# A chunked delta attention: its inverse's last corner closed a wave later, the gates' differences behind the attention rows, the fourth z part by another bank, the norm's product on ScalarE

## The chip, the cores and the metric

The kernel runs on one core of one Trainium2 chip. The metric is the device time of one execution in microseconds, the median of several runs. It computes four small transformer layers in one launch, all in fp32, and only the last layer's attention, here called the delta stage, is touched by the change.

## The reference, cut to what matters

The hidden state has 2 x 512 tokens of 256 features. The delta stage has 16 key heads with two value heads each, dimension 128, and works on blocks of 128 tokens where the reference takes 64:

```python
qkvz = hidden_states @ W_qkvz               # per key head: q 128, k 128, v 2x128, z 2x128
qkv_c = silu(causal_conv(qkv, taps=4))      # per channel
beta = sigmoid(b); g = -exp(A_log) * softplus(a + dt_bias)
# per chunk, per value head:
g_cum = cumsum(g); decay = exp(tril(g_cum[:, None] - g_cum[None, :]))
attn = solve_triangular(I - L, I)           # L = -(k beta) k^T * decay, strictly lower
v_new = attn @ (v beta) - attn @ (k beta exp(g_cum)) @ state
out = (q exp(g_cum)) @ state + ((q k^T) * decay) @ v_new
state = state * exp(g_last) + (k exp(g_last - g_cum))^T @ v_new
# after it, per value head:
xf = out * silu(z); xf = xf * rsqrt(mean(xf*xf) + eps) * norm_weight
y = xf @ W_out                              # summed over heads, added into x
```

## The kernel before, in words

Five engines run programs of their own that meet only at semaphores. The delta stage is one software pipeline of waves: W = 64, wave w is chunk c = w mod 4 (CH = 4 blocks of 128 tokens) of key head h = w // 4, and it covers PR = 4 problems at once (2 batches x 2 value heads). Each engine's loop body (from L2341 for TensorE) is an order written out by hand. In body w before the change:

- for wave w+2, two ahead: `make_scores` (L2087, q and k against k, into bank BK), `turn_values` (L2098) and `turn_keys` (L2104) into bank BT; on VectorE `make_low` (L2635, differences of the gates' sums, from rows that SyncE broadcasts, `load_gates`, L1964), `make_v0` (L2650), `make_at` (L2641), `make_qg` (L2655); on ScalarE `make_decay` (L2409) and `grow` (L2415) are the exponentials, `make_values` and `make_keys` (L2424) the copies.
- `spread` on SyncE (L1970 to L1984) stores v0 and hands its 16x16 diagonal blocks to GpSimd; GpSimd's `substitute` (L2585 to L2598) inverts them in some thirty small steps; `gather` (L1993, L1999) brings them back a wave later.
- for wave w the inverse is put together from those blocks: `widen` (L2663), `join_a` (L2115), `close_wa` (L2671), `close_a` (L2127, L2131), `join_b` (L2140), `close_b` (L2150, L2152) in 32x32 tiles, then `join_c` (L2160) and `close_c` (L2169) for the last 64x64 corner. ScalarE's `copy_whole` (L2445) takes the finished bank BZ to `inv`.
- for wave w-1: `recall` (L2180) with `make_right` (L2690), `ask` (L2203), `solve` (L2192) with `new_values` (L2450), `grow_state` (L2218) with `carry` (L2712; not after a head's last chunk, and recall and ask not in its first), `answer` (L2209), then `gated` (L2700, xf), `square` (L2458), `reduce` (L2719) and on GpSimd `root` (L2567) and `normed` (L2573).
- for wave w-2: `turn_out` (L2229), `copy_out` (L2465), `project_out` (L2242), `add_out` (L2725).
- between them lie parts: the projections of the next head, eight q, k, v parts (L2043) and four z parts (L2053), `parts_of(w)` of them in a wave: 3, 3, 2, 4 for c = 2, 3, 0, 1. They go to banks BG and BK in turn. `conv` (L2618, L2621) and `silu` (L2396) make the next head's q, k, v from them; ScalarE drains z parts by a Silu (L2390).

SyncE's queue in body w: for c = 1, 2 the next weights (`load_qkv` L1818; `load_z` L1822 and `load_out` L1826), then `load_gates(w+3)`, `spread(w+2)`, `gather(w+1)`. Each issue waits in order.

Of the kernel before, what the change touches and what calls it, by code (L numbers as in the profile page):

```python
# [13 lines left out]
ALU = mybir.AluOpType  # L14
# [3 lines left out]
P = 128  # L18
# [1763 lines left out]
def delta_and_looked_up(nc, ps, d, x, xn, norm, looked_up):  # L1782
# [8 lines left out]
    FIRST_ORDER = (1, 0, 2, 3)  # L1791
    F_TILES = WF * B
# [9 lines left out]
    with Stage(nc, "a3") as s:  # L1802
# [50 lines left out]
        wc, z_half, t_half = (s.buf(n, [P, PR, P // 2]) for n in ("wc", "z_half", "t_half"))  # L1853
        inv = s.buf("inv", [P, 2, PR, P])
        at, qg, v_row, k_row = (s.buf(n, [P, 4, PR, P]) for n in ("at", "qg", "v_row", "k_row"))
        state, rest, v_new = (s.buf(n, [P, PR, P]) for n in ("state", "rest", "v_new"))
        xf, sq, xnorm, out_t = (s.buf(n, [P, PR, P]) for n in ("xf", "sq", "xnorm", "out_t"))
# [3 lines left out]
        f_gated = [of[:, :, :].rearrange("p r t -> p (r t)") for of in (xf, xnorm, state, rest)]  # L1861
# [90 lines left out]
        bg_parts = [part for w in range(-2, W + 2) for part in parts_of(w)[0::2]]  # L1952

        with nc.Block() as block:

            @block.sync
            def _(sp):
# [50 lines left out]
                for w in range(-2, W):  # L2008
# [28 lines left out]
            def _(pe):  # L2037
# [9 lines left out]
                def project_z(g, n, to):  # L2047
                    if n == 0:
                        pe.wait_ge(wz_loaded, 16 * g + 16)
                    for i in range(2):  # L2050
                        tt = 2 * n + i
# [6 lines left out]
                def part(w, n):  # L2058
# [3 lines left out]
                    if n % 2 == 0:  # L2062
# [3 lines left out]
                    elif n == 1:  # L2066
                        pe.wait_ge(v0_ready, PR * (w + 3))
                        pe.wait_ge(at_ready, w + 3)
                    else:
                        wait_part(pe, parts[n - 2])  # L2070
                    g, t = parts[n]
                    if t < 8:
                        project(g, t, (BG, BK)[n % 2])
                    else:
                        project_z(g, t - 8, (BG, BK)[n % 2])

                def make_scores(w):
                    before = parts_of(w - 3)
                    if before:
                        wait_part(pe, before[len(before) // 2 * 2 - 1])  # L2080
# [38 lines left out]
                def close_a(w):  # L2119

                    pe.wait_ge(wa_ready, w + 1)
                    if w >= 1:
                        pe.wait_ge(inv_ready, w)
# [32 lines left out]
                def join_c(w):  # L2156

                    pe.wait_ge(th_ready, w + 1)
                    for r in range(PR):
                        mm = pe.matmul(upper(BW)[SECOND, r, :], v0[FIRST, w % 3, r, SECOND], t_half[FIRST, r, :],  # L2160
                                       start=True, stop=True)
                    mm.then_inc(wc_psum, 1)

                def close_c(w):

                    pe.wait_ge(wc_ready, w + 1)
                    pe.wait_ge(zh_ready, w + 1)
                    for r in range(PR):
                        mm = pe.matmul(bank(BZ)[FIRST, r, SECOND], wc[SECOND, r, :], z_half[SECOND, r, :],  # L2169
                                       start=True, stop=True)  # L2170
# [855 lines left out]
```

## Time and profile before

| what | value |
|---|---|
| median of 3 runs | 2034.4 us (2026.47 to 2035.54) |
| the profiled execution | 2028.85 us, of which span 2027.0 us |
| granted TensorE clock, mean | 0.958 of full |
| TensorE busy | 1843.1 us, 91% |
| VectorE, ScalarE, GpSimd busy | 64%, 49%, 53% |
| DMA | 124.42 MB, mean 61 GB/s |

The span counts from the first to the last instruction; the execution's time has 1.8 us around it. The delta stage's loop begins at about 913 us. Busy time doesn't include semaphores and the issue of DMAs. The matmul ends are modelled, so the start of the next instruction is the safer reading of how long a run took.

### The profile page before, as it was taken

How to read it: one execution, taken by the hardware profiler on the slowest of the kernel's cores; microseconds unless marked ns; L12 is line 12 of the kernel's file. 1: busy time of each engine (PE TensorE's matmuls, PEld its weight loads, DVE VectorE, ACT ScalarE, POOL GpSimd, SP SyncE). 2: the span in 40 equal slices, each digit the busy share in tenths (PEclk: the TensorE clock that was granted, in tenths of full speed). 3: DMA queues.
4: the chain of work that ended last, by engine and by line, in shares of the span. 5: the costliest groups of instructions: out<-in, count | busy, mean ns of one | idle time of the engine just before them, and what ended most of it. 6: DMA issues, size and time to landing. Idle time of an engine off the chain costs nothing.

```text
span 2027.0 us, 45825 instructions
## 1 busy us (share of the span) xinstructions
PE 1843.1 (91%) x16855; PEld 1191.5 (59%) x16855; DVE 1287.5 (64%) x2490; ACT 995.4 (49%) x2433; POOL 1077.0 (53%) x2259
## 2 busy tenths in 40 slices
PE   7799997877899896898999999999999999999987
PEld 5422564432243574346777777777777777677775
DVE  2544564695578533627777777777777777777752
ACT  2375232215321452525656656665666566566643
POOL 0521222224100340126887787887878888888873
PEclk7899998998999796999999999999999999999999
DMA  6035422110010632202222222222222222222221
GB/s 157 1 116 156 108 46 53 52 62 1 1 44 7 176 116 88 40 14 56 53 53 64 64 54 54 64 63 55 49 60 54 53 64 64 54 53 64 44 45 32
DMA packets 231181, 124.42 MB, mean 61 GB/s; under 512 B 141360, under 2 KB 210513, under 8 KB 230705
## 3 DMA queue, kind: packets, MB, share of 16 engines
q1 hardware_dynamic: 225008, 111.20, 22.1%
q0 software_dynamic: 5952, 10.29, 2.2%
q8 instruction: 137, 2.24, 0.5%
q14 instruction: 84, 0.68, 0.1%
HBM read 87.94 MB, written 39.74 MB: 63 GB/s over the span
## 4 chain that ended last, share of the span: by engine, by line
PE 23%; POOL 20%; issue 6%; SPq 4%; ACT 3%; DMA 2%; DVE 2%; POOLq 0%; DVEq 0%; ACTq 0%
POOL a_term L2591 8%; POOL a_z L2595 8%; PE ps L2043 5%; PE ps L2053 3%; PE ps L2242 3%; SPq L1976 2%; POOL a_rstd L2567 2%; POOL a_xnorm L2573 2%; PE ps L2273 2%; DMA a_l<-a_v_dram 1%; SPq L1984 1%; PE ps L2229 1%; PE ps L2160 1%; PE ps L2209 1%; PE ps L2283 1%
## 5 line engine op out<-in xcount | busy, mean ns | idle before, releaser
L2591 POOL TENSOR_TENSOR a_term<-a_z,a_l 32x14 f32<-32x14 f32 (+6 forms) x896 | 342.8, 383 | 70.3
L2595 POOL TENSOR_TENSOR a_z<-a_z,a_term 32x14 f32<-32x14 f32 (+6 forms) x896 | 339.6, 379 | 70.2
L2621 DVE SCALAR_TENSOR_TENSOR a_qkv<-a_raw,a_taps,a_qkv 128x1024 f32<-128x1024 f32 x192 | 247.1, 1287 | 6.1
L2043 PE MATMUL ps<-all_xn,a_w_qkv 128*128 128x512 f32 x512 | 246.7, 607 | 0.0
L390 POOL DMA_INDIRECT f_rows<-a_row,a_slots x32 | 35.4, 1105 | 184.6 <-DVE a_of_tile L380 139.2
L2242 PE MATMUL ps<-a_out_t,a_w_out 128*128 128x256 f32 x512 | 130.7, 399 | 1.9 <-ACT a_out_t L2465 1.7
L2043 PEld LDWEIGHTS ps<-all_xn,a_w_qkv 128*128 128x128 f32 x512 | 89.2, 193 | 69.1 <-issue 67.3
L2386 ACT ACTIVATE a_raw<-ps 128x512 f32<-128x512 f32 x128 | 76.4, 598 | 108.2 <-PE ps L2043 107.5
L2053 PE MATMUL ps<-a_w_z,all_xn 128*128 128x256 f32 x512 | 122.6, 383 | 0.0
L2585 POOL COPY a_z<-a_l 32x256 f32<-32x256 f32 x64 | 27.1, 423 | 154.6 <-DMA a_l<-a_v_dram 154.4
L850 POOL DMA_INDIRECT f_sums<-a_y,a_xs x23 | 36.1, 1568 | 136.3 <-ACT a_y L799 133.4
L2242 PEld LDWEIGHTS ps<-a_out_t,a_w_out 128*128 128x128 f32 x512 | 93.8, 193 | 17.8 <-ACT a_out_t L2465 2.3
L2700 DVE SCALAR_TENSOR_TENSOR a_xf<-ps,a_zs 128x512 f32<-128x512 f32 x64 | 44.2, 690 | 91.0 <-POOL a_xnorm L2573 65.5
L2053 PEld LDWEIGHTS ps<-a_w_z,all_xn 128*128 128x128 f32 x512 | 93.6, 190 | 12.7 <-issue 1.2
L2650 DVE SCALAR_TENSOR_TENSOR a_v<-ps,a_gates,a_decay 128x128 f32<-128x128 f32 x256 | 71.6, 340 | 43.0 <-ACT a_decay L2409 43.0
L2450 ACT ACTIVATE a_v_new<-ps,a_gates 128x128 f32<-128x128 f32 x256 | 72.9, 367 | 45.7 <-PE ps L2192 45.7
L2635 DVE SCALAR_TENSOR_TENSOR a_low<-a_gc_rows,a_gates,a_floor 128x128 f32<-128x128 f32 x256 | 87.9, 403 | 1.6 <-DMA a_gc_rows<-a_g_dram 1.6
L630 PE MATMUL ps<-a_w,a_xt 128*128 x184 | 86.6, 593 | 0.6 <-ACT a_xt L779 0.6
L2567 POOL TENSOR_TENSOR a_rstd<-a_var,a_half 128x4 f32<-128x4 f32 x64 | 68.7, 1073 | 22.1 <-DVE a_var L2719 22.1
L772 ACT ACTIVATE a_probs<-ps 128x512 f32<-128x512 f32 x128 | 66.1, 602 | 23.9 <-PE ps L593 23.9
L2445 ACT ACTIVATE a_inv<-ps 128x512 f32<-128x512 f32 x64 | 38.3, 598 | 76.9 <-PE ps L2169 76.9
L2209 PE MATMUL ps<-a_v_new,a_at 128*128 128x128 f32 x512 | 74.8, 290 | 1.2 <-ACT a_v_new L2450 1.2
(331 smaller groups left out, 4304.7 us busy)
## 6 DMA issues: line engine op xcount, KB each, us to landing
a_gc_rows<-a_g_dram SPq DMA_DIRECT2D x64, 256.0 KB, 4.8
a_v_dram<-a_v SPq DMA_DIRECT2D x64, 256.0 KB
a_w<-in_f_w SPq DMA_DIRECT2D x24, 512.0 KB, 4.5
a_w_qkv<-in_a_w SPq DMA_DIRECT2D x16, 512.0 KB, 3.9
a_t_dram<-a_z SPq DMA_DIRECT2D x512, 8.0 KB
a_w_z<-in_a_w SPq DMA_DIRECT2D x16, 256.0 KB, 2.9
a_w_out<-in_a_wo SPq DMA_DIRECT2D x16, 256.0 KB, 3.1
a_v_off<-a_v SPq DMA_DIRECT2D x256, 4.0 KB
```

Source lines behind the costliest of these rows:

```text
L630: mm = pe.matmul(ps[:, bank + i % 2, :], xt[:, i % 2, k, :], w[:, bass.ds(e, 1), first + k * FF:first + (k + 1) * FF], start=k == 0, stop= ...
L2043: mm = pe.matmul(ps[:, to, :], w_qkv[:, k, mt * P:(mt + 1) * P], xn[:, k, b * T:(b + 1) * T], start=k == 0, stop=k == KC - 1)
L2053: mm = pe.matmul(ps[:, to, i * 256:(i + 1) * 256], xn[:, k, tt * P:(tt + 1) * P], w_z[:, k, :], start=k == 0, stop=k == KC - 1)
L2209: mm = pe.matmul(bank(BO)[:, r, :], at[:, w % 4, r, :], v_new[:, r, :], start=w % CH == 0 and r == 0, stop=r == PR - 1)
L2242: mm = pe.matmul(bank(BO)[:, B * m:B * (m + 1), :], w_out[:, v, m * P:(m + 1) * P], out_t[:, v::VPK, :], start=v == 0, stop=v == VPK - 1)
L2386: act.activation(raw[:, mt, b, TAPS - 1:], ps[:, of, :], ACT.Copy).then_inc(raw_ready, 1)
L2450: act.activation(v_new[:, r, :], bank(BR)[:, r, :], ACT.Copy, scale=gate(K_BETA, w, r)).then_inc(vnew_ready, 1)
L2567: pool.tensor_tensor(rstd[:, :], var[:, :], half[:, :], ALU.pow).then_inc(rstd_ready, 1)
L2591: pool.tensor_tensor(term[:, 0:j, j + 1:], z[:, 0:j, j:j + 1].broadcast_to([HP, j, n]), rows[:, j:j + 1, j + 1:].broadcast_to([HP, j, n]), ...
L2595: pool.tensor_tensor(z[:, 0:j, j + 1:], z[:, 0:j, j + 1:], term[:, 0:j, j + 1:], ALU.add).then_inc(sub_step, 1)
L2621: dve.scalar_tensor_tensor(to, rows, tap, to, ALU.mult, ALU.add).then_inc(conv_ready if j == TAPS - 1 else conv_step, 1)
L2635: dve.scalar_tensor_tensor(low[:, r, :], gc_rows[:, w % 2, r, :], gate(K_GC, w, r), floor[:, :], ALU.subtract, ALU.min).then_inc(low_ready, 1)
```

## The change

It does seven things. The closing of the last corner for wave w-1 is interleaved with the joining for wave w (`join_and_close_c`), and `copy_closed` takes only that quarter to `inv`; VectorE's `copy_halves` takes the two diagonal halves there. Everything that needs the inverse runs for w-2, and the output for w-3, so the loop has one more body. `part(w, 0)` stands behind `join_a` in the bodies that grow no state. Part 1 alone uses bank BK, the others BG, and the z parts' order is (0, 2, 1, 3). `make_low` runs for w+3 behind `make_at`. `normed` goes from GpSimd to four ScalarE activations, with xf doubled. `make_keys` goes ahead of `copy_wc`; `load_out` goes from c = 2 to c = 3; in c = 0 the conv's last tap goes to the head of the next body's.

```diff
+    Z_ORDER = (0, 2, 1, 3)
-        bg_parts = [part for w in range(-2, W + 2) for part in parts_of(w)[0::2]]
+        bg_parts = [parts[n] for parts in map(parts_of, range(-2, W + 2)) for n in range(len(parts)) if n != 1]
...
-                    if c == 2 and h >= 1:
+                    if c == 3 and 1 <= h:
                         sp.wait_ge(y_psum, CH * h)
                         load_out(sp, h)
...
+                def join_and_close_c(w):
+                    if made(w):
+                        pe.wait_ge(th_ready, w + 1)
+                    if made(w - 1):
+                        pe.wait_ge(wc_ready, w)
+                        pe.wait_ge(zh_ready, w)
+                    if made(w - 2):
+                        pe.wait_ge(inv_ready, w - 1)
                     for r in range(PR):
+                        if made(w):
+                            begun = pe.matmul(upper(BW)[SECOND, r, :], v0[FIRST, w % 3, r, SECOND],
+                                              corner[FIRST, r, :], start=True, stop=True)
+                        if made(w - 1):
+                            closed = pe.matmul(upper(BW)[FIRST, r, :], corner[SECOND, r, :],
+                                               inv[SECOND, (w - 1) % 2, r, SECOND], start=True, stop=True)
...
-                for w in range(W + 2):
-                    if made(w - 1):
-                        recall(w - 1)
+                for w in range(W + 3):
+                    if made(w - 2):
+                        recall(w - 2)
                     if made(w + 2):
                         make_scores(w + 2)
...
-                    part(w, 0)
+                    if w == W:
+                        join_and_close_c(w)
+                    grows = (w - 2) % CH != CH - 1
+                    if grows:
+                        part(w, 0)
                     if made(w):
                         join_a(w)
-                    if made(w - 1):
-                        grow_state(w - 1)
+                    if not grows:
+                        part(w, 0)
...
                     if made(w):
-                        join_c(w)
-                    if made(w - 2):
-                        project_out(w - 2)
+                        join_and_close_c(w)
+                    if made(w - 3):
+                        project_out(w - 3)
                     part(w, 3)
-                    if made(w):
-                        close_c(w)
...
-                def copy_whole(w):
+                def copy_closed(w):
                     act.wait_ge(c_psum, w + 1)
-                    act.activation(inv[:, w % 2, :, :], bank(BZ), ACT.Copy).then_inc(inv_ready, 1)
+                    act.activation(inv[FIRST, w % 2, :, SECOND], upper(BW)[FIRST, :, :],
+                                   ACT.Copy).then_inc(inv_ready, 1)
...
+                def normed(w):
+                    act.wait_ge(rstd_ready, w + 1)
+                    if w >= 1:
+                        act.wait_ge(ot_psum, w)
+                    for r in range(PR):
+                        of = act.activation(xnorm[:, r, :], xf[:, w % 2, r, :], ACT.Copy, scale=rstd[:, r:r + 1])
+                    of.then_inc(xnorm_ready, 1)
...
                     if made(w):
                         copy_wb(w)
+                    if made(w - 3):
+                        normed(w - 3)
                     part(w, 1)
...
                     if silus:
                         silu(w // CH + 1, 1)
+                    part(w, 2)
+                    if silus:
+                        silu(w // CH + 1, 2)
+                    if made(w + 2):
+                        make_keys(w + 2)
                     if made(w):
                         copy_wc(w)
...
+                    if made(w) and made(w - 1):
+                        copy_closed(w - 1)
                     if silus:
                         silu(w // CH + 1, 3)
...
-                    if made(w - 1):
-                        root(w - 1)
-                        normed(w - 1)
+                    if made(w - 2):
+                        root(w - 2)
...
+                def copy_halves(w):
                     dve.wait_ge(b_psum, w + 1)
-                    dve.tensor_copy(z_half[SECOND, :, :], bank(BZ)[SECOND, :, SECOND]).then_inc(zh_ready, 1)
+                    if w >= 2:
+                        dve.wait_ge(x_psum, w - 1)
+                    for of in (SECOND, FIRST):
+                        cp = dve.tensor_copy(inv[of, w % 2, :, of], bank(BZ)[of, :, of])
+                    cp.then_inc(zh_ready, 1)
...
-                    if made(w + 2):
-                        make_low(w + 2)
-                    if made(w - 1):
-                        make_right(w - 1)
+                    if made(w - 2):
+                        make_right(w - 2)
...
                     if made(w + 2):
                         make_at(w + 2)
+                    if made(w + 3):
+                        make_low(w + 3)
                     if made(w):
                         close_wa(w)
...
+                    if w % CH == 1:
+                        conv(w - 1, 3)
                     conv(w, 0)
...
+                    if w % CH in (1, 3):
                         conv(w, 3)
```

## Rows read from the trace of the kernel before

**Rows 1.** Busy time by stretch: stretch, us, then each engine's busy (xcount), PEclk, DMA.

```profile
942.63:1919.73 977.10, 945.94 (x11930) 705.05 (x11929) 719.51 (x1527) 604.03 (x1653) 799.14 (x1855) 1.00 0.25 57
1919.73:2027.04 107.31, 83.86 (x1226) 69.09 (x1224) 47.46 (x131) 46.75 (x157) 57.53 (x159) 0.94 0.18 40
```

**Rows 2.** TensorE's waits, 942.63 to 1919.73: total us, times, longest.

```profile
PE ps L2229 <- POOL a_xnorm L2573: 8.3, 13, 1.4
PE ps L2098 <- DVE all_x L2725: 6.9, 7, 1.1
```

**Rows 3.** Timeline of TensorE, end of a c=1 wave and the c=2 wave.

```profile
1426.59 0.68 PE L2160 MATMUL ps<-a_t_half,a_v 64*64 64x64 f32 x8
1427.19 1.99 PE L2242 MATMUL ps<-a_out_t,a_w_out 128*128 128x256 f32 x8
...
1429.02 1.89 PE L2053 MATMUL ps<-a_w_z,all_xn 128*128 128x256 f32 x8
1430.84 0.68 PE L2169 MATMUL ps<-a_z_half,a_wc 64*64 64x64 f32 x8
1431.45 1.13 PE L2180 MATMUL ps<-a_state,a_qkv 128*128 128x256 f32 x4
...
1449.23 1.13 PE L2180 MATMUL ps<-a_state,a_qkv 128*128 128x256 f32 x4
```

**Rows 4.** Timeline of TensorE, the 32x32 runs of the same wave.

```profile
1438.08 1.16 PE L2218 MATMUL ps<-a_v_new,a_k_row 128*128 128x128 f32 x8
1439.16 0.45 PE L2127 MATMUL ps<-a_t_wide,a_wa 32*32 32x32 f32 x32
1439.44 0.45 PE L2131 MATMUL ps<-a_wa,a_t_wide 32*32 32x32 f32 x24
...
1440.91 0.44 PE L2140 MATMUL ps<-a_tb,a_v 32*32 32x32 f32 x16
1441.28 1.98 PE L2043 MATMUL ps<-all_xn,a_w_qkv 128*128 128x512 f32 x4
```

**Rows 5.** Timeline of ScalarE, second half of the c=1 wave.

```profile
1424.75 0.69 ACT L2465 ACTIVATE a_out_t<-ps,a_nw 128x512 f32<-128x512 f32 x1 [0.84 <-PE ps L2229]
...
1426.50 1.04 ACT L2396 ACTIVATE a_qkv<-a_qkv 128x1024 f32<-128x1024 f32 x1
1427.57 0.38 ACT L2441 ACTIVATE a_wc<-ps 64x256 f32<-64x256 f32 x1
...
1432.53 1.15 ACT L2424 ACTIVATE a_k_row<-ps,a_gates 128x128 f32<-128x128 f32 x4
1433.69 1.28 ACT L2409 ACT_TABLE_LOAD   x1
```

**Rows 6.** Timeline of GpSimd, the norm's product.

```profile
1439.28 1.04 POOL L2573 TENSOR_TENSOR a_xnorm<-a_xf,a_rstd 128x512 f32<-128x512 f32 x1
```

**Rows 7.** Timeline of VectorE, head of the c=2 wave.

```profile
1432.62 1.13 DVE L2690 SCALAR_TENSOR_TENSOR a_rest<-ps,a_gates,a_v_row 128x128 f32<-128x128 f32 x4 [0.60 <-PE ps L2180]
1435.72 1.13 DVE L2650 SCALAR_TENSOR_TENSOR a_v<-ps,a_gates,a_decay 128x128 f32<-128x128 f32 x4 [1.97 <-ACT a_decay L2409]
...
1437.09 0.69 DVE L2641 TENSOR_TENSOR a_at<-ps,a_decay 128x512 f32<-128x512 f32 x1
```

**Rows 8.** SyncE's issues in a c=0 wave, and the gates' rows' landings.

```profile
1470.53 0.33 SPq L1970 DMA_DIRECT2D a_v_dram<-a_v  x1
...
1483.56 0.41 SPq L1964 DMA_DIRECT2D a_gc_rows<-a_g_dram  x1
DMA to landing us min/median/max: 4.7/4.8/5.0
```

**Rows 9.** Timeline of TensorE, waves 62, 64 and the last answer.

```profile
1985.03 0.45 PE L2115 MATMUL ps<-a_t_wide,a_v_off 32*32 32x32 f32 x32 [2.82 <-DVE a_t_wide L2663]
...
2007.61 1.13 PE L2180 MATMUL ps<-a_state,a_qkv 128*128 128x256 f32 x4
...
2012.35 1.16 PE L2209 MATMUL ps<-a_v_new,a_at 128*128 128x128 f32 x8 [1.23 <-ACT a_v_new L2450]
```

More of the change, by code:

```diff
@@ L2154, in close_b @@
                     mm.then_inc(b_psum, 1)
-                def join_c(w):
-                    pe.wait_ge(th_ready, w + 1)
-                    for r in range(PR):
[L2160 to L2170, printed above, removed]
-                    mm.then_inc(c_psum, 1)
+                def join_and_close_c(w):
[3 more added lines that the diff above has]
+                        pe.wait_ge(wc_ready, w)
+                        pe.wait_ge(zh_ready, w)
+                    if made(w - 2):
+                        pe.wait_ge(inv_ready, w - 1)
+                    for r in range(PR):
+                        if made(w):
[4 more added lines that the diff above has]
+                                               inv[SECOND, (w - 1) % 2, r, SECOND], start=True, stop=True)
+                    if made(w):
+                        begun.then_inc(wc_psum, 1)
+                    if made(w - 1):
+                        closed.then_inc(c_psum, 1)
                 def recall(w):
@@ L2202, in ask @@
                     for r in range(PR):
-                        pe.matmul(bank(BO)[:, r, :], qg[:, w % 4, r, :], state[:, r, :], start=r == 0, stop=False)
+                        pe.matmul(bank(BO)[:, r, :], qg[:, w % 5, r, :], state[:, r, :], start=r == 0, stop=False)
                 def answer(w):
@@ L2208, in answer @@
                     for r in range(PR):
-                        mm = pe.matmul(bank(BO)[:, r, :], at[:, w % 4, r, :], v_new[:, r, :],
+                        mm = pe.matmul(bank(BO)[:, r, :], at[:, w % 5, r, :], v_new[:, r, :],
                                        start=w % CH == 0 and r == 0, stop=r == PR - 1)
@@ L2389, in silu_z @@
                     act.wait_ge(z_ready, 4 * g + n + 1)
-                    act.activation(zs[:, g % 2, 2 * n:2 * n + 2, :].rearrange("p t n -> p (t n)"),
+                    if g >= 2 and n >= 2:
+                        act.wait_ge(xf_ready, CH * (g - 1))
+                    first = 2 * Z_ORDER[n]
+                    act.activation(zs[:, g % 2, first:first + 2, :].rearrange("p t n -> p (t n)"),
                                    ps[:, of, :], ACT.Silu).then_inc(zs_ready, 1)
@@ L2518, in _ @@
                     f_silu(t)
-                for w in range(W + 2):
+                for w in range(W + 3):
                     silus = parts_of(w) if w % CH == 1 else []
@@ L2814, in _ @@
                 f_add(1)
-                for w in range(W + 2):
+                make_low(2)
+                for w in range(W + 3):
                     late = w % CH == 2
-                    if made(w + 2):
-                        make_low(w + 2)
-                    if made(w - 1):
-                        make_right(w - 1)
+                    if made(w - 2):
+                        make_right(w - 2)
                     if made(w + 2):
```

111 lines of the change are left out of this document (53 added, 58 removed).

## The prediction

> **What bounds the kernel now.** I read the busy time by stretches first, then TensorE's waits, then the timelines of one head, engine by engine, and SyncE's queue. Only the delta stage changes. Its loop runs 64 waves, four to a head, and the fourteen heads from wave 2 to wave 58 take 977.1 us, 69.8 a head, at a granted clock of 1.00 [rows 1]. TensorE is busy 945.9 us of that and idle 31.2, or 2.2 a head. So TensorE's instruction stream sets the period, and there are two ways to shorten it: fewer microseconds in the stream, or fewer waits. The waits are small and many: the largest two are for the norm's product on GpSimd (8.3 us in 13 waits) and for the last addition into x (6.9 in 7) [rows 2]. From wave 58 on no projections are left to fill TensorE; it is idle 23 of 107 us and waits for chains through other engines.
>
> Waves are named by c = w mod 4. A wave's start is its first matmul, at 1431.45 for a c=2 wave; it ends at 1449.23, 17.8 long [rows 3]. One projection part is 1.83 (1429.02 to 1430.84 is the last of the c=1 wave before it).
>
> **Part 1, the corner.** Before, joining and closing the 64x64 corner are two runs of eight instructions, each 0.60 to its successor's start, the second at the wave's end: 1426.59 to 1427.19 and 1430.84 to 1431.45 [rows 3]. Now the closing of the wave before runs interleaved with the joining of this one, on the other half of the rows and of the output partitions. Do the halves overlap? The 32x32 runs answer for quarters: 32 instructions over four row groups go by in 0.28 (1439.16 to 1439.44), while 16 over two groups take 0.37 up to a 128-wide one (1440.91 to 1441.28) [rows 4]. Time goes by the instructions of one row group, eight in either case, not by the count. So the merged run should be 0.60 to 0.66; with 0.65 the stream loses 0.56 a wave, **2.2 us a head**. If nothing overlapped, 16 instructions would stand in line and the gain would be the one change of shape, at least 0 and by the 0.37 against 0.28 about 0.1. The Trainium skill (TensorEngine Tiling (Array Packing), Key Properties) says that different tiles can load weights and multiply in parallel, and that a change of tiling mode drains TensorE. These rows agree with the first for quarters; no row shows it for halves. By the page alone the saving would be 0.6 and a little for the drain that goes.
>
> ScalarE's copy of the whole inverse (128x512, 0.5) becomes a copy of a quarter (0.4, as its copy of wc, 1427.57 to about 1427.98 [rows 5]); VectorE copies two halves for one, 0.43 more. VectorE is busy 719.5 of 977.1, 74% [rows 1], so this costs nothing while its order holds.
>
> **Part 2, the shift by a wave.** recall, ask, solve, grow and answer now run for w-2, output for w-3. The work is the same but moves between waves: without waits I get 17.0 for c=3, 15.2 for c=0, 17.7 for c=1 and 15.1 for c=2 (17.8 less 0.3 of waits and 0.56; then c=0 has one part fewer; c=1 has one part more and no grow, 1.08 by 1438.08 to 1439.16 [rows 4]; c=2 has no recall and no ask, 1.9). Sum 65.1; from above, 69.8 - 2.2 - 2.2 = 65.4. I use **65.3**.
>
> **Part 3, the norm.** GpSimd loses 1.04 a wave [rows 6], ScalarE gains four 128x128 products, 1.1 us a wave (its four scaled copies at 1432.53 take 1.15 [rows 5]). The normed tile is now asked for a wave after its root, so the 8.3 us of waits go, and VectorE no longer waits for it before xf. ScalarE was 62% busy (604.0 of 977.1) and goes to about 70%.
>
> **Part 4, the gates' differences.** make_low moves from the wave's head to behind make_at and works a wave ahead. This frees the chain low, decay, v0: v0 was 1.97 late behind decay in the c=2 wave [rows 7]. In full waves v0 is then ready 3.3 after the start: recall to rest 1.17 (1431.45 to 1432.62), rest and v0 1.05 to 1.1 each. But the rows it reads are still fetched by SyncE in the same wave, one wave of slack gone. On SyncE's in-order queue, from v0's first store to the fetch there are 13.0 us (1470.53 to 1483.56) and the landing is 4.7 to 5.0 later [rows 8]: 18.0, and 18.1 with the semaphore. So the rows land 3.3 + 18.1 = 21.4 after a wave's start. VectorE asks for them 4.3 to 4.7 into the next wave (v0 ends at 3.3, then 0.33 and 0.66 [rows 7]), and behind that wait in its queue stand close_wa, qg, za, xf and the convolution; TensorE waits for close_wa. Per wave:
> - c=1 follows the short c=0: 21.4 - 15.2 = 6.2. VectorE is held 1.9, then low 1.25 and close_wa 0.3, so TensorE can close at 7.8. It wants to at 6.4 (1439.16 is 7.7 into its wave; less 1.08 for grow and 0.2 of waits): **1.5 us** waited.
> - c=3 follows c=2 and a fetch of w_out is now ahead on the queue (0.45): 6.1 or so; wanted at 7.4: **0.3**.
> - c=0 lands at 4.1: nothing. c=2 lands by 4.5, but decay waits for a table load of 1.28 behind the last z part [rows 5]: v0 ends at 3.6, low at 5.85, close_wa at 6.2 against 5.7: **0.5**.
>
> **Part 5, the fourth z part by the other bank.** The scores of the c=2 wave no longer wait for its drain. But they need the fourth silu of the conv, and ScalarE's queue ahead of that silu has grown by the keys' copies (1.16) and the quarter's copy (0.4). From turn_out in c=1: 0.65 to copy_out, 1.75 for it and the squares (1424.75 to 1426.50), silu 1.07, z 0.5 (a 128x512 drain, as copy_out), silu 1.07, keys 1.16, wc 0.4, quarter 0.4, silu 1.07 [rows 5]: 8.1. TensorE needs 6.9 from the same point (0.5 for turn_out, 0.3 for the keys' turn, the merged 0.65, and three times 1.83: part, output, part), so the scores wait about **1.0**.
>
> New waits: 1.5 + 0.3 + 0.5 + 1.0 = 3.3 a head. A head is 65.3 + 3.3 = **68.6**, 1.2 less than 69.8; fourteen heads -16.8.
>
> **The ends.** At the front wave 1 has less to do but waits for the same t_wide: -0.6 for its closing. At the end there is one more wave. Before, the join of wave 62 starts at 1985.03, the last full recall at 2007.61, the last answer at 2012.35, and the span ends at 2027.0 [rows 9]. After: 22.6 less two closings of 0.56 is 21.5; then wave 64, which now also grows, answers and projects: 4.7 + 1.1 + 1.1 + 0.5 + 0.8 + 1.9 = 10.1; then 4.7 and 14.7 as before: 51.0 for 42.0, **+9.0**. Waves 58 to 61 are bound by SyncE's 13 us queue and gain only what v0 is earlier, -2.5. Ends together +5.9.
>
> Sum: -16.8 + 5.9 = -10.9. The profiled execution (span 2027.0, time 2028.9) would come to 2016 and 2018; the median of 2034.4 to **2023.5**. Within 0.5%, about what a measurement can tell from no change, is 2024.2 to 2044.6, so the forecast lies on the edge.
>
> **Rivals.**
> 1. *The gates' rows hold nobody.* VectorE reaches make_low later than I think, or the landing hides: then 1.8 of the 3.3 go, 14 x 1.8 = 25, about 1998. For it: SyncE's queue does nothing but issue, and 13.0 could shrink with an earlier v0. Against: it waited for v0 in old waves, so it was not late. If the silu wait goes too: 2023.5 - 46 = 1977.
> 2. *Slower: the gates' rows hold three waves hard.* If SyncE's run takes 15 or more for 13 (it passes the wait for GpSimd's result, which in the short waves ends about when SyncE gets there), each landing is 2 us later and c=1 and c=3 wait 2 more each, less what a longer wave gives back: 14 x 2.3 = 32, 2055. It decides from a landing more than about 5.8 into a full wave.
> 3. *Halves don't overlap.* The 0.56 shrinks to 0.1: 64 x 0.46 = 29, 2053. For it: no row shows halves. Against: [rows 4].
>
> **How the numbers follow.** Forecast, with 2010 to 2036 as its own range (0.9 a head either way): 0.48. Rival 1: 0.18 for 1998, 0.10 for 1977. Rival 2: 0.13. Rival 3: 0.11. Faster by over 0.5%: 0.26 of the forecast's 0.48 and rival 1, 0.54. Within: 0.22. Slower: rivals 2 and 3, 0.24. The range of 8 in 10 is 1985 to 2050.
>
> **What would show it.** A head from 69.8 to 68.6. The merged run 0.65 before its successor; 1.2 refutes part 1. TensorE's wait for close_wa in c=1 waves near 1.5, with VectorE idle before make_low until the gates' rows land; if that idle is absent, part 4 is wrong. TensorE's scores in c=2 waiting about 1 us for ScalarE's silu. No wait for xnorm. One more wave after 63, the last 42 us being about 51. It would be wrong most of all if SyncE's run from v0 to the fetch changed by more than a microsecond, or if a wait I have not placed appears in every wave: 1 us a wave is 60 us.

## The result, and the profile after

The changed kernel is slower: 2047.0 us median of 8 runs (2040.79 to 2056.04) against 2030.95 (2026.47 to 2035.54) for the kernel before on the same chips, a ratio of 1.009 with a 95% interval of 1.007 to 1.011. The forecast was 2023.5. The sign is wrong; the time lies in the range of 8 in 10, near its upper end, and outside the forecast's own range of 2010 to 2036. The profiled execution took 2053.3 us (span 2051.2) at a mean clock of 0.945; it is one of the longer ones, so the differences between the two traces are some 8 us larger than those between the medians. All medians here and below leave out executions that ran in a slower state (two of the ten of experiment 1, one of the ten of experiment 3).

The two answers of the busy time by stretches, as in [rows 1], give the place: the fourteen heads and the rest.

```profile
949.62:1931.99 982.37, 915.42 (x11916) 691.46 (x11916) 726.77 (x1582) 645.49 (x1874) 750.66 (x1792) 0.98 0.26 57
1931.99:2051.20 119.21, 86.65 (x1269) 72.72 (x1268) 50.52 (x139) 57.82 (x203) 48.67 (x152) 0.92 0.16 36
```

| stretch | before | after | measured | forecast |
|---|---|---|---|---|
| loop's first scores to wave 2 | 29.5 | 34.2 | +4.7 | -0.6 |
| fourteen heads | 977.1 | 982.4 | +5.3 | -16.8 |
| from there to the end | 107.3 | 119.2 | +11.9 | +6.5 |
| the loop | 1113.9 | 1135.8 | +21.9 | -10.9 |

Two things stand in the heads' row. TensorE was busy 915 us, thirty less than before, so the stream did get shorter; and its idle time grew from 31 to 67 us. The granted clock is 0.98, where [rows 1] have 1.00. TensorE's waits, 950 to 1930 (total us, times, longest), say for whom:

```profile
PE ps L2130 <- DVE a_wa L2694: 47.4, 38, 3.2
PE ps L2090 <- ACT a_qkv L2413: 14.5, 14, 1.8
PE ps L2239 <- ACT a_xnorm L2486: 3.8, 11, 0.8
```

These are the places that the prediction named: the closing of the 32x32 tiles, behind VectorE's make_low, and the scores of the c=2 wave behind the silu. Their sizes differ. TensorE's timeline of a c=1 wave and the c=2 and c=3 waves after it (start, duration; in brackets the idle time before and its releaser):

```profile
1418.28 1.03 PE L2188 MATMUL ps<-a_state,a_qkv 128*128 128x256 f32 x4
...
1427.07 0.45 PE L2130 MATMUL ps<-a_t_wide,a_wa 32*32 32x32 f32 x32 [2.37 <-DVE a_wa L2694]
...
1439.33 1.10 PE L2090 MATMUL ps<-a_qkv 128*128 128x256 f32 x4 [0.98 <-ACT a_qkv L2413]
1445.58 0.45 PE L2130 MATMUL ps<-a_t_wide,a_wa 32*32 32x32 f32 x32 [0.62 <-DVE a_wa L2694]
1462.43 0.45 PE L2130 MATMUL ps<-a_t_wide,a_wa 32*32 32x32 f32 x32 [0.18 <-DVE a_wa L2694]
```

So 2.4, 0.6 and 0.2 for c=1, 2 and 3, where 1.5, 0.5 and 0.3 were forecast. Over the fourteen heads the c=1 waves wait 31.6 us (1.0 to 3.2 each), the c=3 waves 9.6, c=2 5.1 and c=0 1.5; by the forecast it would be 21, 4, 7 and nothing. The reason behind it on VectorE and SyncE, same waves:

```profile
1425.30 1.52 DVE L2658 SCALAR_TENSOR_TENSOR a_low<-a_gc_rows,a_gates,a_floor 128x128 f32<-128x128 f32 x4 [2.85 <-DMA a_gc_rows<-a_g_dram]
1406.64 0.33 SPq L1975 DMA_DIRECT2D a_v_dram<-a_v  x1
...
1409.69 1.53 SPq L1989 DMA_DIRECT2D a_l<-a_v_dram  x4
1412.08 5.97 SPq L1998 DMA_DIRECT2D a_t_dram<-a_z  x8
...
1420.33 0.41 SPq L1969 DMA_DIRECT2D a_gc_rows<-a_g_dram  x1
```

VectorE stands 2.85 us ahead of make_low until the gates' rows land, 18.7 after v0's first store was issued at 1406.64.

The last reading is about the clock. In the next c=1 wave TensorE waits 2.76, and then runs slowly. Its timeline, and the busy time by stretches of five microseconds there (the column ahead of the DMA share is the granted clock):

```profile
1491.34 1.99 PE L2058 MATMUL ps<-a_w_z,all_xn 128*128 128x256 f32 x8
...
1496.09 0.45 PE L2130 MATMUL ps<-a_t_wide,a_wa 32*32 32x32 f32 x32 [2.76 <-DVE a_wa L2694]
...
1498.75 3.00 PE L2058 MATMUL ps<-a_w_z,all_xn 128*128 128x256 f32 x8
```

```profile
1490.00:1495.00 5.00, 3.33 (x50) 2.61 (x48) 1.95 (x6) 3.02 (x6) 3.92 (x15) 1.00 0.68 209
1495.00:1500.00 5.00, 3.91 (x83) 3.40 (x84) 3.93 (x8) 2.84 (x8) 2.82 (x5) 0.74 0.11 11
1500.00:1505.00 5.00, 5.00 (x58) 3.98 (x59) 3.60 (x6) 3.41 (x14) 4.30 (x10) 0.92 0.12 13
```

A z part of 1.99 takes 3.00: for a few microseconds right after the wait the clock is at its lower level, 1.2 instead of 2.4 GHz. The head with the 2.37 wait has no such stretch. What a stretch costs is seen when the heads are compared one by one, each from its c=2 scores to the next ones. One of before, and three of the changed kernel, without a slow stretch, with a short one and with a long one (length, then TensorE's busy time, and the clock ahead of the DMA share):

```profile
1083.79:1153.62 69.83, 67.56 (x853) 50.37 (x853) 51.36 (x110) 43.18 (x119) 56.58 (x132) 1.00 0.25 58
```

```profile
1090.86:1158.91 68.05, 64.25 (x852) 48.61 (x853) 52.19 (x113) 46.29 (x135) 54.35 (x128) 1.00 0.26 59
1158.91:1229.89 70.98, 65.86 (x852) 49.75 (x853) 51.79 (x113) 46.18 (x135) 55.36 (x134) 0.98 0.25 56
1509.90:1580.76 70.86, 67.40 (x852) 50.86 (x853) 51.73 (x113) 46.22 (x135) 55.61 (x134) 0.95 0.27 57
```

The same matmuls (852 or 853 in the records) keep TensorE busy for 64.3 us in the heads at full clock (five of the fourteen), 65.9 in those at 0.98 (seven) and 67.3 in those at 0.95 (two): 1.6 and 3.0 more, 17 in all. Before, all fourteen have a clock of 1.00 and 67.6. The waits alone don't explain the result, then; the experiments take the two apart.

### The profile page after: what moved, and what is told of

Its sections match the earlier page's. It is cut to its first block, busy times and chain, and to the rows that moved or that the text cites. A ratio compares the mean times of both kernels' runs of the same rounds, so it can differ in the third digit from the quotient of the medians.

```text
span 2051.2 us, 46269 instructions
## 1 busy us (share of the span) xinstructions
PE 1816.9 (89%) x16855; PEld 1181.4 (58%) x16855; DVE 1297.9 (63%) x2555; ACT 1045.7 (51%) x2689; POOL 1022.3 (50%) x2195
## 4 chain that ended last, share of the span: by engine, by line
PE 16%; POOL 12%; SPq 10%; DMA 9%; ACT 7%; issue 5%; DVE 4%; POOLq 0%; DVEq 0%; ACTq 0%
POOL a_z L2619 5%; DMA a_gc_rows<-a_g_dram 5%; POOL a_term L2615 5%; SPq L1998 4%; PE ps L2048 3%; SPq L1981 3%; PE ps L2058 2%; DMA a_t_dram<-a_z 2%; PE ps L2219 2%; PE ps L2283 2%; DVE a_low L2658 1%; SPq L1989 1%; PE ps L2252 1%; ACT a_qkv L2413 1%; DVE a_v L2673 1%
## 5 line engine op out<-in xcount | busy, mean ns | idle before, releaser
L2048 PE MATMUL ps<-all_xn,a_w_qkv 128*128 128x512 f32 x512 | 251.2, 617 | 0.0
L2609 POOL COPY a_z<-a_l 32x256 f32<-32x256 f32 x64 | 33.9, 529 | 222.7 <-DMA a_l<-a_v_dram 222.7
L2058 PE MATMUL ps<-a_w_z,all_xn 128*128 128x256 f32 x512 | 134.6, 410 | 0.0
L2673 DVE SCALAR_TENSOR_TENSOR a_v<-ps,a_gates,a_decay 128x128 f32<-128x128 f32 x256 | 71.7, 340 | 66.0 <-ACT a_decay L2426 65.9
L2058 PEld LDWEIGHTS ps<-a_w_z,all_xn 128*128 128x128 f32 x512 | 100.5, 204 | 16.0 <-issue 1.2
L2446 ACT ACTIVATE a_tb<-ps 96x128 f32<-96x128 f32 x64 | 17.5, 273 | 138.6 <-PE ps L2134 138.6
L2486 ACT ACTIVATE a_xnorm<-a_xf,a_rstd 128x128 f32<-128x128 f32 x256 | 81.3, 391 | 12.6 <-POOL a_rstd L2599 12.3
L2219 PE MATMUL ps<-a_v_new,a_at 128*128 128x128 f32 x512 | 81.2, 306 | 1.2 <-ACT a_v_new L2470 1.2
L2708 DVE COPY a_inv<-ps 64x256 f32<-64x256 f32 x128 | 54.0, 422 | 42.3 <-PE ps L2155 40.3
```

The lines of the kernel that those rows point to most:

```text
L2048: mm = pe.matmul(ps[:, to, :], w_qkv[:, k, mt * P:(mt + 1) * P], xn[:, k, b * T:(b + 1) * T], start=k == 0, stop=k == KC - 1)
L2058: mm = pe.matmul(ps[:, to, i * 256:(i + 1) * 256], xn[:, k, tt * P:(tt + 1) * P], w_z[:, k, :], start=k == 0, stop=k == KC - 1)
L2219: mm = pe.matmul(bank(BO)[:, r, :], at[:, w % 5, r, :], v_new[:, r, :], start=w % CH == 0 and r == 0, stop=r == PR - 1)
L2486: of = act.activation(xnorm[:, r, :], xf[:, w % 2, r, :], ACT.Copy, scale=rstd[:, r:r + 1])
L2673: dve.scalar_tensor_tensor(v0[:, w % 3, r, :], bank(BK)[:, 2 * (r // VPK) + 1, :], gate(K_NBETA, w, r), decay[:, r, :], ALU.mult, ALU.mult ...
```

## The experiments

The theory: the gates' rows land late, TensorE waits for close_wa, and the slow stretches follow from that wait. The rivals: the wait is there but something else is due next, so that its removal brings little; the slow stretches have another cause (the load, the new order); and the loss is in one of the other parts. Each is compared with the kernel before, measured beside it; two experiments differ in time only where their intervals don't overlap.

**1. The gates' rows fetched a wave earlier.** The fetch goes from ahead of `spread` to behind it, for w+4, so nothing waits behind it for a landing and it has a wave more.

```diff
+                load_gates(1)
...
-                    if made(w + 3):
-                        load_gates(w + 3)
                     if made(w + 2):
                         spread(w + 2)
+                    if made(w + 4):
+                        load_gates(w + 4)
```

> The changed kernel with one edit: SyncE fetches the gates' rows for wave w+4 behind spread(w+2), instead of those for w+3 ahead of it. The fetch is then issued some 8 us after a wave's start and lands at 13, and VectorE asks for it 20 us or more after that start. Theory 1 (the late landing holds VectorE, TensorE idles, and the granted clock halves after the longest of these idles): TensorE's waits for close_wa (47.4 us in 38 times between 950 and 1930) all but vanish, the loop's clock is 1.00 throughout, a head takes 66.5 or less for 70.1, and the time is 2047 - 50 = 1997, some 0.983 of the kernel before. Rival 2 (the clock falls because of the new order itself, whoever waits): the waits go, the spells at half clock between 1000 and 1900 stay, head 67.5, about 2010, 0.99. Rival 3 (another wait takes its place, above all join_a for t_wide because SyncE's queue is as long as before): time 2035 or more.

Measured: 2013.7 us, 0.992 (0.988 to 0.996), the loop 1100.9 us. TensorE's waits, 950 to 1930:

```profile
PE ps L2240 <- ACT a_xnorm L2487: 29.0, 19, 2.9
PE ps L2091 <- ACT a_qkv L2414: 14.4, 14, 1.7
PE ps L2131 <- DVE a_wa L2695: 7.5, 14, 0.8
```

The wait for close_wa falls from 47.4 to 7.5 us and the loop is 35 shorter, so the landing is shown as the main cause: this one edit turns slower into faster. But part of the gain is taken by a wait that had been hidden, for the norm's product, which stands behind GpSimd's root. 1997 wasn't reached. Nor is the clock at 1.00 throughout: three slow stretches are left in the heads, each behind a wait of 2.5 to 2.9 for that product. The number is nearest to rival 2's 2010, but its condition isn't met, since most of the stretches went with the waits.

**2. Only make_low back at the wave's head.** The other way to give the fetch its slack.

```diff
-                make_low(2)
                 for w in range(W + 3):
+                    if made(w + 2):
+                        make_low(w + 2)
...
-                    if made(w + 3):
-                        make_low(w + 3)
```

> The changed kernel with make_low back at the head of each wave for w+2, nothing else undone. The gates' rows have their wave of slack again, but decay and with it v0 come 1.3 to 1.6 us later in every wave. Theory 1: no VectorE wait for the rows; TensorE's waits for close_wa shrink to those of the kernel before (6.3 us) or little more, the clock holds at 1.00 in the loop, about 2005 to 2012. If the move of make_low was worth its own gain (v0 earlier), this is 5 to 15 us slower than the early fetch; if it is equal, the move bought nothing. Rival 2: about 2020, spells at half clock stay.

Measured: 2021.8, 0.994 (0.992 to 0.997), the loop 1104.2. It also cures the wait for close_wa, and has in its place one of 14.0 us in 24 for `rest` and a smaller one for the norm's product (12.5 us in 10); the one for the silu stays (11.8 in 12). Two slow stretches are left in the heads. 2005 to 2012 was missed, and the intervals of the two cures overlap, so that their times don't tell which is better. As delivered, then, part 4 costs more than it brings: without it the rest of the change is faster than before.

**3. The wait kept, TensorE kept busy in it.** Five idle matmuls of 128x256 into a bank nobody reads, ahead of close_a in each c=1 wave. If the slow stretches come from the wait, they go and the kernel gets faster, though it does more.

```diff
+                    if w % CH == 1 and made(w - 2) and made(w):
+                        for _ in range(5):
+                            pe.matmul(ps[:, BH, 256:512], ident[:, :], xn[:, 0, 0:256], start=True, stop=True)
                     if made(w):
```

> The changed kernel plus five matmuls of 128x256 (2.3 us at full clock) into an unused half of a PSUM bank ahead of close_a in every c=1 wave, where TensorE waits 2.2 to 3.2 us for close_wa. The wait itself stays, only TensorE isn't idle in it. Theory 1 with the clock as a part of the loss: the spells at half clock between 1000 and 1900 (eight, of 3.4 or 6.8 us in the trace) go, and with them some 1.7 us each: 2047 - 15 = 2032. Rival (the clock has nothing to do with these waits): no change or up to 10 us slower where the wait was shorter than 2.3.

Measured: 2035.0, 1.003 (1.001 to 1.005), 12 less than the change's median. Busy time by stretches, of this kernel and then of the changed kernel:

```profile
1500.00:1800.00 300.00, 288.21 (x3789) 218.00 (x3788) 226.76 (x497) 197.18 (x577) 231.36 (x553) 1.00 0.27 58
```

```profile
1500.00:1800.00 300.00, 280.89 (x3544) 212.20 (x3543) 217.17 (x472) 197.42 (x568) 226.44 (x542) 0.96 0.26 57
```

The wait for close_wa is down to 19.0 us in 30, the filler stands in its place, and the clock is at 1.00 in all fourteen heads. The slow stretches follow the idle of the wait, not the load or the new order.

**4. The same wait in the kernel before.** The change isn't in it. Six chained memsets of a scratch tile hold VectorE ahead of close_wa in fourteen c=1 waves.

```diff
+                    if w % CH == 1 and 4 <= w < W - 6:
+                        for n in range(6):
+                            before = 6 * (w // CH - 1) + n
+                            if before:
+                                dve.wait_ge(held, before)
+                            dve.memset(scratch[:, :], 0.0).then_inc(held, 1)
                     if made(w):
```

> The kernel before with six fills of a scratch tile (0.5 to 0.6 us each, one after the other) on VectorE ahead of close_wa in fourteen c=1 waves; nothing else. VectorE is 3.0 to 3.6 later there, TensorE waits some 2.3 to 2.9 for close_wa. Theory with the clock: spells at half clock appear behind these waits, as in the changed kernel, some 1.7 us each: 14 x 2.6 = 36 us of waits and 10 to 20 more, 2075 to 2085. Rival (the wait costs itself alone): no spells in the loop, 2065 or less.

Measured: 2101.7, 1.034 (1.031 to 1.037), 69.4 more, 5.0 a wave. TensorE's waits (1000 to 1900; before they were 5.9 us in 13), its timeline in one of the waves, and the busy time of one head:

```profile
PE ps L2129 <- DVE a_wa L2673: 41.5, 24, 3.0
```

```profile
1456.09 0.65 PE L2129 MATMUL ps<-a_t_wide,a_wa 32*32 32x32 f32 x32 [2.97 <-DVE a_wa L2673]
...
1457.08 2.08 PE L2211 MATMUL ps<-a_v_new,a_at 128*128 128x128 f32 x8
```

```profile
1096.85:1172.17 75.32, 70.28 (x853) 52.57 (x853) 54.09 (x116) 43.17 (x119) 56.11 (x133) 0.95 0.22 54
```

Of the 5.0, 3.0 is the wait and what is left, 2.0, comes after it: the answer, 1.16 in [rows 9], takes 2.08, and the clock over the loop falls to 0.96 without anything of the change. By the traces' heads the mean idle time rises from 2.2 to 4.8 us and the busy time from 67.6 to 70.1. All fourteen waits were followed by a slow stretch. More was lost than I expected, because I had priced the stretch too low: twelve of the fourteen are of the long kind, with a clock of 0.95 in their head.

**5. The second silu earlier.** Experiment 1, and silu(1) right behind silu(0) on ScalarE: the queue ahead of the last silu is 1.1 shorter after the last part.

```diff
                         silu(w // CH + 1, 0)
+                        silu(w // CH + 1, 1)
...
-                    if silus:
-                        silu(w // CH + 1, 1)
```

> The early fetch, and in c=1 waves the second conv silu right behind the first, so that ScalarE's queue ahead of the fourth is 1.07 shorter. The c=2 scores waited 0.98 for that silu in each head. If ScalarE's queue is what they wait for: that wait goes, 14 x 1.0 = 14 us less than the early fetch alone, about 1983. If the silu's place delays copy_wb or normed instead, close_b or turn_out wait in c=1 for as much: equal to the early fetch.

Measured: 2006.5, 0.987 (0.981 to 0.992), the loop 1097.7. The wait of the scores falls from 14.4 us in 14 to 1.8 in 1, which shows that it was ScalarE's queue that made it. The wait for the norm's product is now 31.2 in 28, and five slow stretches stand in the heads. The time is 7 less than experiment 1's where 14 were expected, and the two intervals overlap: that the step gains time isn't shown.

**6. The root inside the substitution.** On top of 5: GpSimd does root(w-2) ahead of the tenth step of substitute(w+2), not behind all of them.

```diff
                     for j in range(1, SB - 1):
+                        if j == 10 and rooted is not None:
+                            root(rooted)
...
-                        substitute(w + 2)
-                    if made(w - 2):
+                        substitute(w + 2, w - 2 if made(w - 2) else None)
+                    elif made(w - 2):
                         root(w - 2)
```

> The early fetch with the early silu, and GpSimd takes the norm's root inside the substitution (before its tenth step) instead of behind it. With the early fetch TensorE came to wait for the normed tile (29 to 33 us between 950 and 1930), and ScalarE's product for the root. Theory: the root stands behind a substitution that ends some 8 to 10 us into the next wave, about when ScalarE wants it; taken 4 to 5 us earlier, these waits go: 20 to 30 us less, about 1980, 0.976 of the kernel before. Rival: the variance itself comes late, GpSimd then stands in the middle of the substitution, and t_wide comes late: no gain or a loss.

Measured: 1992.8, 0.981 (0.979 to 0.984). Measured once more:

> The same kernel as e_root_inside, beside the one with fillers on the same chip: 0.981 of the kernel before if the first measurement holds.

Measured: 1989.1, 0.9805 (0.979 to 0.982); the loop 1075.0 us, 39 less than before and 61 less than the change as delivered, by the traces. It was to be 0.976. TensorE's waits, 950 to 1900, and the busy time by stretch:

```profile
PE ps L2119 <- DVE a_t_wide L2688: 13.1, 12, 1.9
PE ps L2131 <- DVE a_wa L2696: 7.9, 18, 0.5
PE ps L2240 <- ACT a_xnorm L2487: 7.4, 16, 0.8
```

```profile
1000.00:1800.00 800.00, 778.30 (x10289) 588.60 (x10288) 625.47 (x1364) 557.31 (x1621) 654.92 (x1545) 1.00 0.28 60
```

This version beats both kernels. The wait for the norm's product falls from 31.2 us in 28 to 7.4 in 16, and ScalarE's own for the root, 32.8 in 15 in experiment 5, isn't listed any more. So GpSimd's root was late because it stood behind the whole substitution. One slow stretch is left in the heads. The intervals of experiments 5 and 6 overlap a little; those of 1 and 6 don't.

**7. The norm's product back on GpSimd.** Experiment 5 with part 3 undone.

```diff
-                    if made(w - 3):
-                        normed(w - 3)
...
+                def normed(w):
+                    pool.wait_ge(rstd_ready, w + 1)
+                    if w >= 1:
+                        pool.wait_ge(ot_psum, w)
+                    pool.tensor_tensor(xnorm[:, :, :], xf[:, w % 2, :, :],
+                                       rstd[:, :].unsqueeze(2).broadcast_to([P, PR, P]), ALU.mult
+                                       ).then_inc(xnorm_ready, 1)
...
                         root(w - 2)
+                        normed(w - 2)
```

> The early fetch with the early silu, with the norm's product back on GpSimd behind the root. If taking 1.04 us from GpSimd's queue is a part that pays: GpSimd needs 15.4 + 1.04 = 16.4 a wave, more than the short waves' 15.2, xnorm comes a microsecond later, and the time rises by 10 to 20 us over the early fetch with the early silu. If ScalarE's 1.1 us a wave cost as much as GpSimd's did: equal or faster.

Measured: 2050.6, 1.008 (1.006 to 1.011), 44 more than experiment 5. TensorE's wait, and the busy time by stretch, of this kernel and of experiment 5's:

```profile
PE ps L2240 <- POOL a_xnorm L2603: 59.7, 28, 4.5
```

```profile
950.00:1900.00 950.00, 881.65 (x11458) 662.30 (x11458) 714.37 (x1517) 553.84 (x1582) 773.80 (x1765) 0.97 0.26 56
```

```profile
950.00:1900.00 950.00, 908.69 (x11932) 684.67 (x11932) 726.50 (x1583) 646.01 (x1877) 755.20 (x1796) 0.99 0.27 58
```

Part 3 is worth much more than I had put on it, in this order of the loop; in the kernel before, with the product on GpSimd too, the wait was 8.3 us. Here the wait grows by 28 us and the clock falls again; that the latter makes the other 16 was not tried apart.

**8. The merged run taken apart.** Experiment 5 with the four joining matmuls first and the four closing ones behind them.

```diff
+                    for r in range(PR):
                         if made(w - 1):
```

> The early fetch with the early silu, with the four joining matmuls first and the four closing ones behind them instead of in turn. The same 16 instructions. If the halves overlap because instructions of different row halves stand in turn: the run goes from 0.62 to about 1.08 up to its successor (16 x 0.058 + 0.15), 0.46 a wave, and the time rises by up to 64 x 0.46 = 29 us. If the overlap doesn't hang on the turn: no change.

Measured: 2017.2, 0.992 (0.990 to 0.995), 10.7 more than experiment 5. TensorE's timeline:

```profile
1456.59 0.50 PE L2172 MATMUL ps<-a_corner,a_v 64*64 64x64 f32 x5
1456.87 0.27 PE L2176 MATMUL ps<-a_inv,a_corner 64*64 64x64 f32 x1
...
1457.10 0.45 PE L2176 MATMUL ps<-a_inv,a_corner 64*64 64x64 f32 x5
1457.48 0.70 PE L2254 MATMUL ps<-a_out_t,a_w_out 128*128 128x256 f32 x2
```

In a row the sixteen instructions take 0.89 (1456.59 to 1457.48), of which only the last three of the first kind lie beside the second kind. Interleaved, in the changed kernel:

```profile
1415.82 0.27 PE L2171 MATMUL ps<-a_corner,a_v 64*64 64x64 f32 x1
1415.83 0.27 PE L2174 MATMUL ps<-a_inv,a_corner 64*64 64x64 f32 x1
...
1416.29 0.22 PE L2174 MATMUL ps<-a_inv,a_corner 64*64 64x64 f32 x1
1416.45 1.99 PE L2252 MATMUL ps<-a_out_t,a_w_out 128*128 128x256 f32 x8
```

0.63, and the halves overlap. The intervals of the two times overlap as well (0.990 to 0.995, 0.981 to 0.992), so the 10.7 by itself is no proof. The busy time of a head at full clock is one, in experiment 5 and here:

```profile
1083.03:1149.38 66.35, 64.29 (x853) 48.65 (x853) 51.88 (x113) 45.94 (x134) 54.23 (x128) 1.00 0.27 60
```

```profile
1083.79:1151.44 67.65, 65.10 (x853) 49.81 (x853) 52.19 (x113) 46.01 (x134) 55.14 (x131) 1.00 0.29 59
```

It is 0.8 more a head in every such head, 0.2 a wave and 13 us in 64 waves, about half of the 29 that the expectation set as its limit.

**9. Filler at the ends.** Experiment 6 with filler matmuls in waves 0, 1, 61 and 62 and ahead of each late grow, where TensorE waits and the clock is low.

```diff
+                    fill({0: 2, 1: 8, 61: 1, 62: 6}.get(w, 0))
                     if made(w):
                         join_a(w)
...
+                    fill(1 if w >= 58 else 0)
                     if made(w - 2):
                         grow_state(w - 2)
+                    fill({0: 2}.get(w, 0))
```

> The kernel with early fetch, early silu and the root inside the substitution, plus filler matmuls of 128x256 (0.46 us each) into an unused half of a bank where TensorE idles at the loop's two ends: four in wave 0, eight in wave 1 ahead of join_a (idle 4.4 there), one each from wave 58 on ahead of grow_state, six in wave 62. Theory: the spells at half clock at both ends (some 10 us of them in waves 0 and 1, 20 after wave 57) become fewer, 1.7 us each: 4 to 10 us less than without the fillers. Rival: they only lengthen the ends where the idle is shorter than they are: no change or up to 5 slower.

Measured: 1988.9, 0.980 (0.978 to 0.981), which is experiment 6's 1989.1. The last stretch, with the filler and without:

```profile
1850.00:1985.00 135.00, 116.20 (x1687) 96.13 (x1672) 71.95 (x183) 78.31 (x263) 73.84 (x207) 0.96 0.18 36
```

```profile
1850.00:1985.00 135.00, 109.18 (x1548) 91.44 (x1542) 68.66 (x173) 76.26 (x256) 68.86 (x192) 0.94 0.18 36
```

The clock is a little higher and nothing is gained: the rival was right. A filler paid in the heads, where the stream sets the time, and not at the ends, where, as I read it, chains through other engines do.

**10. make_low at the head, once the fetch is early.** Experiment 6 with the edit of experiment 2.

```diff
-                make_low(2)
                 for w in range(W + 3):
+                    if made(w + 2):
+                        make_low(w + 2)
...
-                    if made(w + 3):
-                        make_low(w + 3)
```

> The kernel with early fetch, early silu and the root inside, with make_low back at the head of the wave. Now the gates' rows hold nobody in either place, so the difference is what make_low's move is worth by itself. Theory: v0 is ready up to 1.3 us earlier with the move, SyncE's queue and GpSimd start earlier, and t_wide, for which TensorE waits 19 us in the loop, comes earlier: without the move 10 to 20 us slower, about 2007. If v0's time doesn't matter: no change.

Measured: 2002.8, 0.987 (0.985 to 0.989), 13.7 more than experiment 6. TensorE's waits, 950 to 1900:

```profile
PE ps L2201 <- DVE a_rest L2719: 14.4, 26, 2.2
```

So part 4's idea is good for some 14 us, as expected, provided the rows it reads come a wave earlier. The wait that it spares is the one for `rest`, which VectorE makes ahead of make_low when that is moved; I had expected the one for t_wide, which is smaller here (5.9 in 17 for 13.1 in 12). The listed waits don't add up to the 14, being no longer in sum than experiment 6's. Most of it is in the busy time, 0.8 a head, of experiment 6 and of this kernel:

```profile
1075.87:1140.99 65.12, 64.24 (x852) 48.63 (x853) 51.44 (x113) 45.94 (x134) 53.99 (x130) 1.00 0.28 62
```

```profile
1082.86:1149.76 66.90, 65.04 (x853) 48.72 (x853) 52.38 (x114) 46.39 (x134) 54.06 (x130) 1.00 0.28 60
```

It stands in the runs around `solve`, which needs `rest`; short waits that the modelled ends of the matmuls cover would look like this, but that is a reading and not shown.

## Why the prediction was wrong, point by point

Two steps failed: a wait was priced at its own length, with the granted clock taken as 1.00 throughout, where the slow stretches behind the waits cost 17 us in the heads (see the sum); and the wait for close_wa was sized at 32 us, where it came to 47 (part 4).

- **Part 1, right.** The merged run was to take 0.65 and takes 0.63; rival 3, halves that don't overlap, falls by the timelines of experiment 8. That the joining and closing matmuls alternate is needed for it.
- **Part 2, the stream, right in direction.** A head at full clock keeps TensorE busy for 64.3 us, where I had 65.3; with the first head, which is shorter, that is 16 us in the change's favour. Why the stream is shorter than forecast was not looked into.
- **Part 3, right and too small.** The waits for the norm's product fall from 8.3 to 3.8 and don't go quite. In experiments 1 and 5 that wait comes back, up to 31 us, for the root on GpSimd, which I had not followed: moving the product off GpSimd left the root behind its substitution.
- **Part 4, the mechanism right and the size wrong.** The step that failed is "18.0, and 18.1 with the semaphore". In the wave shown the landing came 18.7 after the store, and the run on SyncE's queue took 13.7 for 13.0. What lengthens it there is the wait for GpSimd's result: the issue at 1412.08 stands 0.9 behind the end of the four reads (1411.22), where in the wave of [rows 8] it follows them at once (1475.15 after 1475.10). The short wave ahead took 14.9 for 15.2, and make_low 1.52 for 1.25. Together this is the 0.9 by which the wait is longer than the 1.5 forecast. Besides, one run, from a c=0 wave, stood for all four. In the trace of before the means are 13.0, 14.9, 12.7 and 12.7 for stores in c=0, 1, 2 and 3; after the change they are 13.6, 18.4, 13.3 and 14.2. In the run behind a c=1 store SyncE waits for the place of the next z weights, 54.8 us in 14 for 12.9 in 10; that one is followed by the small waits of c=2. In many waves the store of v0 now starts right behind the gates' fetch, and the read of v_dram waits for that store's landing (below). The wait for close_wa came to 47.4 us for the 32 of my sum.
- **Part 5, right.** 0.98 for 1.0, 14.5 us in fourteen; experiment 5 shows its cause. (8.1 less 6.9 is 1.2; it was rounded down.)
- **The ends, wrong by 5 each.** In front the waits are 1.40 for close_wa in wave 0 and 3.79 for t_wide in wave 1, and parts take 3.3 to 3.7 for 1.9, at a mean clock of 0.85 where it was 1.00. In the tail, from the join of wave 62 on it is 53.0 us, 11.0 more than before where I had 9.0. Ahead of it, waves 58 to 61 lose 0.9 where I had 2.5 gained: close_wa waits 3.04 at 1955.92, in a stretch that I had taken as bound by SyncE's queue. The long wait in wave 1 (1.41 before) is in every kernel with the new order, 3.8 to 6.6 us where no filler stands in it. How much of the two ends is the shift by a wave itself was not tried.
- **The sum, where the sign was lost.** It took every microsecond at the granted clock of 1.00 that [rows 1] show, and priced a wait at its own length. Against 960.3 forecast for the heads, 982.4 is 22.1 more: +15 of waits for close_wa, +0.5 for the scores, +5 for the norm's product and the rest, +17 for the slow clock, -16 for the shorter stream. The clock is the largest and has no term in the prediction; the mis-sized waits come next. Without either of the two the heads would have gained. Experiments 3 and 4 show the clock's part from both sides, experiment 1 that of the waits.
- **The rivals.** The second, the slower one, is nearest to what happened: its place is right, and its point of decision, 5.8 into a full wave, was just passed (the rows of the c=3 wave land 5.95 into it). Its price (2.3 a head for a queue of 15) was of the wrong kind: the waits for close_wa cost 1.1 a head over the forecast, and the clock 1.2. It had too little of the chance.

SyncE's waits, 950 to 1930, for the fourth point:

```profile
SPq L1989 <- DMA a_v_dram<-a_v: 31.8, 25, 2.7
SPq L1998 <- POOL a_z L2622: 19.6, 20, 2.1
```

Before, the first isn't among SyncE's waits in the heads, and the second was 4.0 in 9. Both stand between v0's store and the next gates' fetch.

What stays open: why a wait is followed by a slow stretch in some heads and not in others, and what the extra wave costs by itself. The length of the wait doesn't decide it alone. In the changed kernel's heads the nine stretches stand behind waits for close_wa of 1.6 to 3.2 us, while six c=1 waits of 1.0 to 2.4 have none; in experiment 1 two of 2.6 and 2.8 have none, in experiment 7 two of 3.2.

## What to carry to other kernels

When an edit takes a wave of slack from a fetch, follow the queue in both directions, and give the fetch its slack back before timing the edit: here one moved issue was the difference between 1.009 and 0.992, and two more moves made it 0.98. Where a dense TensorE stream sets the time, a single wait of nearly 3 us can cost its length and then 1.6 to 3.0 us of lost work more; the best version's trace has no wait over 1.9 us in its heads, and one slow stretch in them for the changed kernel's nine. Each wait removed shows the next one, so read the waits again after every edit.

## What the runs showed of the hardware

- The granted clock fell to 1.2 GHz right behind single waits in a stream that is busy before and behind them. In the kernel before with VectorE held, all fourteen waits of about 3.0 us were followed by it, at 2.0 us each beyond the wait. In the changed kernel nine waits of 1.6 to 3.2 were, and others as long as 2.4 were not; a stretch cost 1.6 us of TensorE's time in a head with a mean clock of 0.98, and 3.0 in one with 0.95. The Trainium skill (TensorE: Matmul & The Clock Gate, Part 1: The HAM clock gate) says that the clock is cut when TensorE has not been active enough of late; the fourteen of fourteen agree, and the price is the runs'.
- Sixteen 64x64 matmuls on the two halves in alternation take 0.63 us, as long as eight (0.60); in a row they take 0.89. The order of issue decides the overlap here.
- The landing of v0's store is waited for 31.8 us in 25 of the changed kernel's waves, up to 2.7 each, and wasn't waited for before. Where the 256 KB broadcast fetch of the gates' rows stands behind it (experiment 1) it is 1.5 in 3, but with the same order in experiment 6 it is 13.2 in 13. That the fetch ahead of the store makes it was not tried alone and isn't shown.
